# State-space stage of a twelve-stage decoder: the scan's input formed by differences, 1/A moved, boundary inputs apart

## The chip, the cores and the metric

The kernel runs on one core of a Trainium2 chip. The metric is the device time of one execution in microseconds (us): the median of three runs of the kernel before is 1734.0 us (1726.0 to 1737.9). One more execution was profiled; it took 1747.2 us.

## The reference

Twelve post-norm stages follow each other over x of 8 batches x 256 tokens x 128 dimensions. The change touches the seventh, a selective state-space layer with N = 16 states per dimension:

```python
BC = x @ W_in + b_in
Bm, Cm = (BC[..., :N], BC[..., N:])
dt = jax.nn.softplus((x @ W_dt1 + b_dt1) @ W_dt2 + b_dt2)
dt = jnp.clip(dt, 1e-07, 1000000.0)
tmp = A * dt[..., None]
A_bar = jnp.exp(tmp)
B_barX = jnp.expm1(tmp) / tmp * dt[..., None] * Bm[:, :, None, :] * x[..., None]

def combine(e1, e2):
    a1, b1 = e1
    a2, b2 = e2
    return (a1 * a2, a2 * b1 + b2)
_, h = jax.lax.associative_scan(combine, (A_bar, B_barX), axis=1)
return jnp.sum(h * Cm[:, :, None, :], axis=-1) + D * x
...
x = _layernorm(x + _L2_attn_ref(x, L2_attn_W_in, L2_attn_b_in, L2_attn_W_dt1, L2_attn_b_dt1, L2_attn_W_dt2, L2_attn_b_dt2, L2_attn_A, L2_attn_D), axis=-1)
```

So h(t) = a(t) h(t-1) + (a(t) - 1)/A B(t) x(t) for each dimension and state, with a = exp(A dt), and y sums C h over the 16 states.

## The kernel before

Each engine has its own hand-written program, and stages are Python functions named after the layer (L1f is the gated layer ahead, L2a the state-space stage, L2x the attention behind). Engines meet through counting semaphores; every engine runs its program strictly in the written order.

**The stage L2a.** Work is cut into 32 chunks t = 4 b + c: batch b, and four of the 16 states (c). A chunk is a tile of 128 dimensions x 1024, that is 4 states x 256 tokens. For each chunk:

- ScalarE (`scan_scaled`, L2475) multiplies the batch's tokens by the B of four states: eight 128x128 instructions. TensorE (`scan_inputs`, L1810) transposes them into PSUM banks 0-1 or 2-3, so that dimensions lie on partitions.
- ScalarE (`decays`, L2515 and L2516) writes a = exp(A dt) and tanh(A dt / 2), four instructions of 256 columns each. With them a - 1 is (a + 1) times the tanh.
- VectorE (`feed`, L3376) forms (a + 1) B x out of PSUM, GpSimd (`scan_gains`, L854 and L855) clears the decay of each first token and multiplies by the tanh.
- VectorE scans (L3384, both inputs in SBUF) and multiplies by C (L3388), which TensorE has spread over the partitions into banks 4-5 (`spread_c`, L1896: a 16-row selection matrix `SEL` times the rows of C, in fp32). Banks 4-5 exist once: chunk t's C is spread only after chunk t-1's product.
- TensorE sums the states into bank 6 (`summed`, L1912: eight matmuls of 128 columns against `by_state`, the identity over A) and adds D x (L1907). At the end of a batch VectorE reads y and adds x (`residual`, L3393), takes moments, GpSimd the root, and VectorE normalises (L3408).

**Preparation of a batch** runs inside the chunks of the two batches before it: transpose x (L1785), copy (L2435), project to C and to the low rank (L1790, L1791), copy with bias (L2445, L2446), step sizes and B (`scan_step_sizes`, L1796 and L1798), then on VectorE `scan_sized` (L3265, L3268: B and z), on ScalarE exp(-|z|) (L2453, L2455) and squares (L2462), on VectorE a series for softplus (L3275, L3278) and the clip (L3299, L3300). All of it passes through bank 7. Batches 0 and 1 are prepared inside L1f, between its own steps. The constants SCAN_... say at which chunk of the loop each piece stands; `due(t, offset, 4)` picks the batch.

The order on TensorE in the loop over chunks is: the inputs of chunk t + 2, the preparation due, C of chunk t, the sum of chunk t - 1. The order on VectorE is: feed of chunk t + 1, scan and product of chunk t, then the pieces due.

## Time and profile before

| | |
|---|---|
| median of 3 runs | 1734.0 us |
| profiled execution | 1747.2 us, of which the span is 1745.5 us |
| first scan of L2a starts | 765.1 us |
| reads of y, first to last batch | 799.5 to 973.1 us |
| VectorE, ScalarE, TensorE busy, 780 to 967 us | 177.1, 172.0, 173.5 of 187.0 us |

Times inside the profile are microseconds from the start of the span. PE is TensorE (PEld its weight loads), DVE VectorE, ACT ScalarE, POOL GpSimd. A float32 matmul stands as two records, one that reads fp32r as one, and a transpose as one. A row's `xN` counts instructions; the length of a timeline row covers all of them, and neighbours on one engine overlap by their start-up. Behind `|` a group row has busy us, the mean ns of one, and how long the engine stood idle before them, with what released it. PEclk is TensorE's granted clock as a share of 2.4 GHz; its two levels are 2.4 and 1.2 GHz.

### The profile page before, as it was taken

Reading aid. Unit: us, or ns where it says so; the run is one execution under the profiler, and the core shown is the slowest. Engines: PE = TensorE matmul, PEld = TensorE weight load, DVE = VectorE, ACT = ScalarE, POOL = GpSimd, SP = SyncE. Lnnn points to the kernel's source line nnn. Section 1 sums busy time; section 2 is a strip of 40 time slices with the busy share of each in tenths; the row PEclk is TensorE's granted clock in tenths of the full one; section 3 lists DMA queues with packets and bytes.
Section 4 is the critical chain, followed back from the end, with each engine's and each line's share of the span. In section 5 each row is a group of like instructions: output and inputs, shape, how many; then the busy total and the mean of one; then the engine's idle time right before and its main releaser. Section 6 shows DMA issues by size and latency. Waiting matters only on the chain.

```text
span 1745.5 us, 34465 instructions
## 1 busy us (share of the span) xinstructions
PE 1524.6 (87%) x12731; PEld 1091.4 (63%) x12741; DVE 1272.4 (73%) x2817; ACT 1068.0 (61%) x2219; POOL 693.3 (40%) x801
## 2 busy tenths in 40 slices
PE   6588778799998898899899999998889999989975
PEld 5344446578877555668678767665548984755542
DVE  2688862697775898479999677758854448758988
ACT  4499942367765676389999155547754443147765
POOL 3456536578887022356767313230000111511223
PEclk9799989899999999988988999999989998799985
DMA  3200121200000000010000100000000000000000
GB/s 133 111 13 14 42 87 39 59 10 2 1 1 1 2 2 2 4 37 1 2 1 1 58 2 2 2 13 2 1 2 1 1 1 11 0 19 2 2 1 25
DMA packets 14791, 30.94 MB, mean 18 GB/s; under 512 B 1537, under 2 KB 10145, under 8 KB 13857
## 3 DMA queue, kind: packets, MB, share of 16 engines
q1 hardware_dynamic: 13602, 26.63, 4.4%
q0 software_dynamic: 1024, 2.10, 0.4%
q8 instruction: 104, 1.70, 0.4%
q14 instruction: 61, 0.50, 0.1%
HBM read 22.42 MB, written 6.29 MB: 16 GB/s over the span
## 4 chain that ended last, share of the span: by engine, by line
PE 48%; ACT 14%; DVE 13%; POOL 13%; issue 11%; DMA 1%; another core or an unknown queue 0%; SPq 0%; POOLq 0%; DVEq 0%; ACTq 0%
PE PS L1420 5%; PE PS L1473 4%; ACT big L2262 4%; POOL big L837 4%; PE PS L1745 3%; DVE negmax L2803 3%; PE PS L1734 3%; POOL big L825 3%; ACT big L2240 2%; POOL big L833 2%; PE PS L1912 2%; PE PS L1495 2%; PE PS L1896 2%; PE PS L1325 2%; PE PS L1399 2%
## 5 line engine op out<-in xcount | busy, mean ns | idle before, releaser
L2240 ACT ACTIVATE big<-PS 128x1024 f32<-128x1024 f32 (+1 forms) x256 | 249.4, 975 | 160.3 <-PE PS L1427 159.8
L2803 DVE TENSOR_REDUCE negmax<-PS 128x4 f32<-128x1024 f32 x192 | 234.7, 1223 | 59.6 <-PE PS L1420 54.7
L1420 PE MATMUL PS<-KS,QS 32*128 32x256 f32 (+1 forms) x1152 | 134.4, 318 | 33.9 <-DVE negmax L2803 20.4
L1420 PEld LDWEIGHTS PS<-KS,QS 32*128 32x128 f32 x1152 | 88.0, 188 | 108.0 <-ACT big L2240 75.8
L711 POOL TENSOR_TENSOR rstd<-veps,mhalf 128x2 f32<-128x2 f32 x72 | 51.4, 714 | 241.3 <-DVE veps L2677 231.8
L1427 PE MATMUL PS<-QS,KS 32*128 32x256 f32 (+1 forms) x1152 | 134.7, 321 | 1.4 <-ACT big L2240 1.4
L1473 PE MATMUL PS<-big,V 128*32 128x256 f32 (+1 forms) x2048 | 134.9, 382 | 0.0
L737 POOL TENSOR_TENSOR res<-resb,XB 128x256 f32<-128x256 f32 x24 | 17.5, 728 | 254.7 <-ACT resb L2326 254.7
L779 POOL TENSOR_SCALAR KT<-QT 128x1024 f32<-128x1024 f32 x64 | 66.7, 1042 | 64.8 <-DVE QT L2822 62.9
L2822 DVE SCALAR_TENSOR_TENSOR QT<-PS,wint 128x1024 f32<-128x1024 f32 x64 | 77.3, 1219 | 16.1 <-PE PS L1365 15.5
L1427 PEld LDWEIGHTS PS<-QS,KS 32*128 32x128 f32 x1152 | 85.4, 188 | 5.5 <-issue 3.7
L825 POOL TENSOR_SCALAR big<-big,rsum 128x256 f32<-128x256 f32 (+1 forms) x144 | 61.2, 438 | 65.2 <-DVE rsum L2724 64.8
L2417 ACT ACTIVATE QT<-PS,W 128x256 f32<-128x256 f32 x128 | 53.5, 471 | 54.3 <-PE PS L1734 54.3
L837 POOL TENSOR_TENSOR big<-big 128x512 f32<-128x512 f32 x64 | 81.3, 1271 | 5.0
L1469 PE MATMUL PS<-big,V 128*32 128x512 f32 x512 | 63.4, 614 | 21.3 <-ACT big L2262 13.7
L1473 PEld LDWEIGHTS PS<-big,V 128*32 128x32 f32 x2048 | 54.4, 110 | 44.0 <-issue 15.3
L1129 PE MATMUL PS<-OT,W 128*128 128x256 f32 x272 | 74.5, 395 | 6.9 <-ACT QT L2188 6.9
L2188 ACT COPY QT<-PS 64x256 f32<-64x256 f32 x128 | 47.0, 367 | 53.3 <-DVE big L2708 51.7
L1912 PE MATMUL PS<-On,V 128*128 128x128 f32 x512 | 78.8, 319 | 0.0
L2262 ACT ACTIVATE big<-KT,W 128x1024 f32<-128x1024 f32 x64 | 73.0, 1141 | 8.9 <-POOL KT L779 8.9
L1912 PEld LDWEIGHTS PS<-On,V 128*128 128x128 f32 x512 | 73.1, 228 | 8.3 <-issue 8.3
L1896 PE MATMUL PS<-OT,SEL 16*128 16x256 f32 x256 | 67.0, 403 | 12.0 <-DVE V L3388 10.9
(479 smaller groups left out, 4331.5 us busy)
## 6 DMA issues: line engine op xcount, KB each, us to landing
W<-in_wpack SPq DMA_DIRECT2D x1, 4180.0 KB, 14.0
W<-in_wpack SPq DMA_DIRECT2D x1, 2560.0 KB, 8.9
W<-in_wpack SPq DMA_DIRECT2D x1, 2449.5 KB, 8.1
y_rows<-one_more SPq DMA_DIRECT2D x1, 2048.0 KB, 10.4
masks<-in_mask SPq DMA_DIRECT2D x8, 256.0 KB, 2.8
x_rows<-x_tok SPq DMA_DIRECT2D x16, 128.0 KB, 2.1
W<-in_wpack SPq DMA_DIRECT2D x1, 1538.0 KB, 6.1
x_tok<-in_x SPq DMA_DIRECT2D x1, 1024.0 KB, 5.0
```

The costliest lines, as they stand in the source:

```text
L825: ins = nc.gpsimd.tensor_scalar(PRW[:, u % 4, c0:c1], PRW[:, u % 4, c0:c1], rsum[:, u % 16, j:j + 1], 1.0, ALU.mult, ALU.mult)
L837: nc.gpsimd.tensor_tensor(q, q, RTW[:, u % 4, :, :], ALU.add).then_inc(sem("t_rope"), 1)
L1129: mm = nc.tensor.matmul(PS[:, QKB[u % 2], k * S:(k + 1) * S], w(f"{n}_w{x}", h * P, (h + 1) * P), OT[:, b, :], start=True, stop=True)
L1420: mm = nc.tensor.matmul(PS[:, MAXB[half], o], QS[r, bm % 2, tm, j * P:(j + 1) * P], KS[r, bm % 2, tm, k], start=not a.causal, stop=last)
L1427: mm = nc.tensor.matmul(PS[:, exp_banks(ge)[half], o], KS[r, be % 2, te, kb * P:(kb + 1) * P], QS[r, be % 2, te, q], start=not a.causal, s ...
L1473: mm = nc.tensor.matmul(out_rows[:, skip:S], v, PX[:, T % 2, h, kb * S:(kb + 1) * S - skip], start=first, stop=last)
L1896: mm = nc.tensor.matmul(PS[:, CB + k // 2, (k % 2) * S:(k % 2 + 1) * S], SEL[:, 4 * c + k, :], C_rows(b), start=True, stop=True)
L1912: mm = nc.tensor.matmul(PS[:, YB, j * P:(j + 1) * P], chunk("h", t)[:, at:at + P], by_state[:, 4 * c + k, :], start=False, stop=c == 3 and ...
L2240: nc.scalar.activation(PX[:, T % 2, 2 * p:2 * p + 2, 0:cols], PS[:, exp_banks(g)[0]:exp_banks(g)[0] + 2, 0:cols], ACT.Exp, scale=a.scale). ...
L2262: nc.scalar.activation((PX, PX2)[k][:, T % 2, 2 * p:2 * p + 2, :], clipped((QT, KT)[k], g), ACT.Exp, scale=a.scale, bias=w(("high_base", " ...
L2803: ins = nc.vector.tensor_reduce(negmax[:, h:h + 2, :].rearrange("p h j -> p (h j)"), banks.rearrange("p h (j k) -> p (h j) k", j=2), AX.X, ...
L2822: nc.vector.scalar_tensor_tensor(clipped(QT, g), PS[:, pair_banks(g):pair_banks(g) + 2, :], -100.0 / a.scale, capT[:, g // PAIRS % 2, :].u ...
```

## The change

The recurrence is rewritten. With v(t) = B(t) x(t), the sum w(t) = A h(t) + v(t+1) obeys w(t) = a(t) w(t-1) + v(t+1) - v(t), so the scan takes the plain decay and the differences of v, and y is the sum over states of (C/A) w minus x(t+1) times the sum over states of C(t) B(t+1) / A. Part by part:

- The tanh (16 a batch on ScalarE), the feed (4 a batch on VectorE) and GpSimd's product are gone. The scan reads its second input from PSUM banks 0-3, directly.
- The scaling of tokens 128 to 255 moves to GpSimd (`scan_scaled`, one 128x512 product a chunk); ScalarE keeps four of the eight.
- `scan_inputs` multiplies by `L2a_ahead` (difference of neighbouring tokens) instead of transposing: eight real float32 matmuls of 128 columns. It now waits for the scan of chunk t - 2, not for the feed, and stands last in TensorE's loop.
- The columns at tokens 127 and 255, which the matrix cannot form, and the first state are computed once a batch (three small matmuls in `scan_turn_x`, two small products on GpSimd in `scan_signed`, two in `scan_first_state`, one decay on ScalarE); `start(t)`, a ScalarE copy of 128x4x2, writes them into PSUM ahead of each scan. It stands behind the scaling and the decays in ScalarE's loop.
- 1/A moves into `SEL`, which has 64 rows (high and low parts of C and of 1/A) in fp32r and is built by VectorE in `scan_constants`; GpSimd's building of the old `SEL` at the start of the kernel goes. `summed` uses the identity as weights: four matmuls of 256 columns.
- C, B and the low rank come from one projection (`L2a_front`); ScalarE copies three pieces of it, and VectorE's new `scan_crossed_rows` makes the low part of C and C(t) B(t+1). `scan_step_sizes` overwrites that bank and so waits for it. z is written by ScalarE.
- At a batch's end: `cross` (matmul), `crossed_inputs` (VectorE), `read_y` (VectorE, in the place of the residual), `result` (two transposes) and `copy_result` (ScalarE), then the moments as before. The D x term carries x too.

```diff
+SCAN_START, SCAN_CROSS, SCAN_Y, SCAN_OUT, SCAN_STATS, SCAN_DONE = -2, 2, 4, 6, 7, 8
...
+                nc.gpsimd.tensor_tensor(chunk("x", t)[:, 512:1024].rearrange("p (k d) -> p k d", k=4),
+                                        x_tok[:, 2 * b + 1, :].unsqueeze(1).broadcast_to([P, 4, D]),
+                                        B_cols(b)[:, 16 + 4 * c:20 + 4 * c].unsqueeze(2).broadcast_to([P, 4, D]), ALU.mult)\
+                  .then_inc(sem("L2a_xs_second"), 1)
...
+                nc.gpsimd.tensor_tensor(starts(b)[:, 0:16], first_decay(b), starts(b)[:, 0:16], ALU.mult).then_inc(own, 1)
...
+                    nc.tensor.matmul(PS[:, 7, S:S + 32], x_tok[0:2, 2 * (b - 1), :], signed_B, start=True, stop=True)
+                    nc.tensor.matmul(PS[:, 7, S + 32:S + 48], x_tok[:, 2 * (b - 1), :], last_B, start=True, stop=False)
+                    mm = nc.tensor.matmul(PS[:, 7, S + 32:S + 48], x_tok[0:1, 2 * b - 1, :], B_cols(b - 1)[0:1, 16:32],
+                                          start=False, stop=True)
...
+                nc.tensor.matmul(PS[:, 7, 0:S], w("L2a_front"), xN(b), start=True, stop=True).then_inc(sem("L2a_psum"), 1)
 
             def scan_step_sizes(b):
-                pe.wait_ge(sem("L2a_bc"), b + 1)
-                nc.tensor.matmul(PS[:, 7, 0:S], w("L2a_wdt2", rows=64), low_rank, start=True, stop=True)
+                pe.wait_ge(sem("L2a_bc"), 2 * b + 2)
+                pe.wait_ge(sem("L2a_rows"), 2 * b + 1)
...
-                    pe.wait_ge(sem("L2a_fed"), t - 1)
...
+                    pe.wait_ge(sem("L2a_scan"), t - 1)
+                for k in range(8):
+                    bank, first = (0, 2)[t % 2] + k // 4, (k // 2 % 2) * S + (k % 2) * P
+                    mm = nc.tensor.matmul(PS[:, bank, first:first + P], chunk("x", t)[:, (k % 2 * 4 + k // 2) * P:(k % 2 * 4 + k // 2 + 1) * P],
+                                          w("L2a_ahead"), start=True, stop=True)
...
-                        mm = nc.tensor.matmul(PS[:, CB + k // 2, (k % 2) * S:(k % 2 + 1) * S], SEL[:, 4 * c + k, :], C_rows(b),
+                        mm = nc.tensor.matmul(PS[:, CB + k // 2, (k % 2) * S:(k % 2 + 1) * S], SEL[:, 4 * c + k, :], C_parts(b),
...
+                        nc.tensor.matmul(PS[:, YB, 0:S], diag, xN(b), start=True, stop=False)
+                    for k in range(4):
+                        mm = nc.tensor.matmul(PS[:, YB, 0:S], ident, chunk("h", t)[:, k * S:(k + 1) * S],
+                                              start=False, stop=c == 3 and k == 3)
+                    mm.then_inc(sem(f"{n}_summed"), 1)
...
+                    nc.tensor.matmul(PS[:, 7, 0:S], w_rows(f"{n}_AT", 32, 48), CB_rows(b), start=True, stop=True)\
+                      .then_inc(sem(f"{n}_turned_out"), 1)
...
+                        mm = nc.tensor.transpose(PS[:, result_bank(b), S + j * P:S + (j + 1) * P], summed_x[:, j * P:(j + 1) * P], ident)
...
+                for k in range(4):
+                    i = 4 * c + k
+                    ins = nc.scalar.activation(chunk("x", t)[:, k * P:(k + 1) * P], x_tok[:, 2 * b, :], ACT.Copy,
+                                               scale=B_cols(b)[:, i:i + 1])
...
+                        ins = nc.scalar.activation(chunk("decay", t)[:, k * S + 1:(k + 1) * S], step_size(b)[:, 1:S], ACT.Exp,
+                                                   scale=w(f"{n}_A", i, i + 1))
...
+                def start(t):
+                    b, c = t // 4, t % 4
+                    act.wait_ge(sem(f"{n}_xB"), t + 1)
...
+                    nc.scalar.copy(PS[:, bank:bank + 2, :].rearrange("p a c -> p (a c)").rearrange("p (k c) -> p k c", k=4)[:, :, 0:P:P - 1],
+                                   starts(b)[:, 16:48].rearrange("p (v k) -> p k v", v=2)[:, 4 * c:4 * c + 4, :])\
+                      .then_inc(sem(f"{n}_started"), 1)
...
+            def scan_crossed_rows(b):
+                dve.wait_ge(sem("L2a_bc"), 2 * b + 2)
...
+                nc.vector.scalar_tensor_tensor(CB_rows(b)[:, 0:S - 1], PS[32:48, 7, 1:S], w_rows("L2a_bfront", 32, 48),
+                                               CB_rows(b)[:, 0:S - 1], ALU.add, ALU.mult).then_inc(sem("L2a_rows"), 1)
...
+                        scan_crossed_rows(0)
...
-                scan_states(6, 16)
...
-                def feed(t):
-                    dve.wait_ge(sem(f"{n}_decay"), t + 1)
...
-                    nc.vector.scalar_tensor_tensor(fed_to(t), chunk("decay", t), 1.0, flat(PS[:, bank:bank + 2, :]),
-                                                   ALU.add, ALU.mult).then_inc(sem(f"{n}_fed"), 1)
...
-                    nc.vector.tensor_tensor_scan(h, chunk("decay", t), chunk("gain", t), 0.0, ALU.mult, ALU.add)\
+                    h, bank = chunk("h", t), (0, 2)[t % 2]
+                    nc.vector.tensor_tensor_scan(h, chunk("decay", t), flat(PS[:, bank:bank + 2, :]), 0.0, ALU.mult, ALU.add)\
...
+                def crossed_inputs(b):
+                    dve.wait_ge(sem(f"{n}_turned_out"), 2 * b + 1)
+                    nc.vector.tensor_tensor(crossed[:, 0:S - 1], PS[:, 7, 0:S - 1], xN(b)[:, 1:S], ALU.mult)\
+                      .then_inc(sem(f"{n}_y_read"), 1)
...
+                    nc.vector.tensor_tensor(summed_x, PS[:, 6, 0:S], crossed, ALU.subtract).then_inc(sem(f"{n}_y_read"), 1)
```

What TensorE runs over one and a half chunks in the middle of the stage, before: C (L1896), sums (L1912), inputs (L1810) and step sizes (L1796, L1798).

```order
L1896 MATMUL PS<-OT,SEL 128x256 [waits L2a_hc,L2a_bc]
L1896 MATMUL PS<-OT,SEL 128x256 x3
L1912 MATMUL PS<-On,V 128x128 [waits L2a_hc]
L1912 MATMUL PS<-On,V 128x128 x7
L1810 MATMUL PS<-W,QT 128x128 [waits L2a_fed,L2a_xs]
L1810 MATMUL PS<-W,QT 128x128 x7
L1796 MATMUL PS<-OT,W 128x256 [waits L2a_bc]
L1798 MATMUL PS<-W,KT 128x16 x2
L1896 MATMUL PS<-OT,SEL 128x256 [waits L2a_hc]
L1896 MATMUL PS<-OT,SEL 128x256 x3
```

And after, from C (L1977) of one chunk on: D x (L1987), sums (L1989), step sizes (L1877, L1879), inputs (L1891).

```order
L1977 MATMUL PS<-KS,SEL 128x256 [waits L2a_hc]
L1977 MATMUL PS<-KS,SEL 128x256 x3
L1987 MATMUL PS<-KT 128x256 [waits L2a_y_read,L2a_hc]
L1989 MATMUL PS<-V,W 128x256 x4
L1877 MATMUL PS<-OT,W 128x256 [waits L2a_rows,L2a_bc]
L1879 MATMUL PS<-W,KT 128x16 x2
L1891 MATMUL PS<-W,QT 128x128 [waits L2a_scan,L2a_xs_second,L2a_xs]
L1891 MATMUL PS<-W,QT 128x128 x7
L1977 MATMUL PS<-KS,SEL 128x256 [waits L2a_hc]
L1977 MATMUL PS<-KS,SEL 128x256 x3
L1989 MATMUL PS<-V,W 128x256 [waits L2a_hc]
```

The inputs stand behind the step sizes now and wait for L2a_scan where they waited for L2a_fed; the sums are four wide matmuls, and L1877 waits for L2a_rows too.

In L1f, around the step sizes of batch 1, TensorE ran this before (L1844 narrows and L1834 widens the gated layer, L1796 and L1798 are the step sizes):

```order
L1844 MATMUL PS<-big,QT 128x128 [waits var,L1f_h]
L1844 MATMUL PS<-big,QT 128x128 x5
L1834 MATMUL PS<-QT,big 128x256 [waits L1f_h]
L1834 MATMUL PS<-QT,big 128x256 x2
L1796 MATMUL PS<-OT,W 128x256 [waits L2a_bc]
L1798 MATMUL PS<-W,KT 128x16 x2
L1834 MATMUL PS<-QT,big 128x256 [waits L1f_silu,xT]
L1834 MATMUL PS<-QT,big 128x256 x2
L1844 MATMUL PS<-big,QT 128x128 [waits var,L1f_h]
```

And it runs this after (L1925, L1915; L1877 and L1879 are the step sizes):

```order
L1925 MATMUL PS<-big,QT 128x128 [waits var,L1f_h]
L1925 MATMUL PS<-big,QT 128x128 x5
L1915 MATMUL PS<-QT,big 128x256 [waits L1f_h]
L1915 MATMUL PS<-QT,big 128x256 x2
L1877 MATMUL PS<-OT,W 128x256 [waits L2a_rows,L2a_bc]
L1879 MATMUL PS<-W,KT 128x16 x2
L1915 MATMUL PS<-QT,big 128x256 [waits L1f_silu,xT]
L1915 MATMUL PS<-QT,big 128x256 x2
L1925 MATMUL PS<-big,QT 128x128 [waits var,L1f_h]
```

Only the wait for L2a_rows is new. It is given by L3402, the second row of `scan_crossed_rows`, which stands on VectorE in L1f behind the gated product (L3466), the rest of the series (L3422) and the clip (L3451, L3452):

```order
L3466 TENSOR_TENSOR QT<-QT,PS 128x768 [waits y,L1f_silu,L1f_h_psum]
L3422 SCALAR_TENSOR_TENSOR xs<-masks,xs 128x256 [waits L2a_q]
L3422 SCALAR_TENSOR_TENSOR xs<-masks,xs 128x256 [waits L2a_q,t_dve]
L3451 SCALAR_TENSOR_TENSOR OT<-OT,xs 128x256 [waits L2a_series]
L3452 SCALAR_TENSOR_TENSOR KT<-OT,KT 128x256 [waits t_dve]
L3400 SCALAR_TENSOR_TENSOR KS<-PS,W,KS 32x256 [waits L2a_bc]
L3402 SCALAR_TENSOR_TENSOR one_more<-PS,W,one_more 16x255
L3410 TENSOR_TENSOR rt<-PS,W 128x32 [waits L2a_psum]
```

Nothing moved past it; the two rows L3400 and L3402 were put between the clip and `scan_sized` (L3410).

ScalarE's order over one chunk after the change: the four scalings (L2583), the decays (L2626), the start copy (L2636), then z (L2561, L2562) and exp(-|z|) (L2564).

```order
L2583 ACTIVATE QT<-x_tok,rt 128x128 [waits L2a_xB,L2a_rows]
L2583 ACTIVATE QT<-x_tok,rt 128x128 x3
L2626 ACTIVATE big<-KT,W 128x255 [waits L2a_scan]
L2626 ACTIVATE big<-KT,W 128x255 x3
L2636 COPY PS<-KT 128x4x2 [waits L2a_xB]
L2561 ACTIVATE KT<-PS,W 128x256 [waits L2a_dt,L2a_series,L2a_rows]
L2562 ACTIVATE OT<-PS,W 128x256
L2564 ACTIVATE KT<-KT 128x256 [waits L2a_u]
L2583 ACTIVATE QT<-x_tok,rt 128x128 [waits L2a_xB]
```

The start copy of the next chunk can be reached only behind the z of this one, which waits for L2a_rows from VectorE.

## Rows read from the trace of the kernel before

**Rows 1.** Engine busy time by stretch; the first row names the columns
```profile
core 0: us, PE busy (x) PEld busy (x) DVE busy (x) ACT busy (x) POOL busy (x), PEclk, DMA share, GB/s
780.00:807.00 27.00, 27.00 (x141) 22.89 (x141) 24.11 (x27) 25.87 (x74) 17.58 (x10) 0.76 0.01 2
...
860.00:887.00 27.00, 23.02 (x146) 18.35 (x145) 25.81 (x30) 25.86 (x74) 18.24 (x11) 0.99 0.00 1
...
780.00:967.00 187.00, 173.49 (x1008) 143.98 (x1008) 177.12 (x189) 172.00 (x489) 130.81 (x72) 0.90 0.00 1
```

**Rows 2.** Groups by line, 800 to 950 us: operation, shapes, count, busy us, mean ns, idle
```profile
L2475 ACT ACTIVATE QT<-x_tok,rt 128x128 f32<-128x128 f32 x186 | 56.6, 386 | 0.0
...
L3384 DVE TENSOR_TENSOR_SCAN V<-big 128x1024 f32<-128x1024 f32 x23 | 52.5, 2283 | 0.0
...
L1896 PE MATMUL PS<-OT,SEL 16*128 16x256 f32 x184 | 48.6, 406 | 7.7 <-DVE V L3388 7.7
...
L3376 DVE SCALAR_TENSOR_TENSOR one_more<-big,PS 128x1024 f32<-128x1024 f32 x12 | 14.6, 1217 | 4.2 <-ACT big L2516 4.2
...
L3278 DVE SCALAR_TENSOR_TENSOR xs<-masks,xs 128x256 f32<-128x256 f32 x20 | 12.7, 636 | 0.5
```

**Rows 3.** Timeline: start us, length us, engine, line, operation, count, idle before
```profile
855.30 2.28 DVE L3384 TENSOR_TENSOR_SCAN V<-big 128x1024 f32<-128x1024 f32 x1
...
855.50 4.23 POOL L855 TENSOR_TENSOR big<-big,one_more 128x1024 f32<-128x1024 f32 x1
...
859.37 0.42 ACT L2453 ACTIVATE KT<-OT 128x256 f32<-128x256 f32 x1 [1.04 <-DVE OT L3268]
```

**Rows 4.** Timeline, the reads of y of the first, sixth and last batch
```profile
799.51 0.42 DVE L3393 TENSOR_TENSOR res<-PS,x_tok 128x256 f32<-128x256 f32 x1
...
933.81 0.42 DVE L3393 TENSOR_TENSOR res<-PS,x_tok 128x256 f32<-128x256 f32 x1
...
973.05 0.42 DVE L3393 TENSOR_TENSOR res<-PS,x_tok 128x256 f32<-128x256 f32 x1 [2.72 <-PE PS L1912]
```

**Rows 5.** Chain that ended last, in order of time: start us, length us, what
```profile
741.95 1.30 PE PS L1834 x6
...
780.41 3.61 PE PS L1912 x16
...
784.02 0.88 PE PS L1810 x8
785.11 1.92 PE PS L1896 x8
787.03 1.98 PE PS L1912 x16
...
863.90 0.40 ACT big L2516
```

**Rows 6.** Timeline of TensorE, matmuls in fp32r (four row tiles of 32 rows)
```profile
1000.24 0.73 PE L1325 MATMUL PS<-HL,spread_by 32*128 32x256 f32 x8
```

**Rows 7.** Timeline, the gated stage ahead, where the first two batches are prepared
```profile
728.45 0.24 DVE L3292 RECIPROCAL negmax<-W 128x16 f32<-128x16 f32 x1
...
733.61 0.70 PE L1796 MATMUL PS<-OT,W 64*128 64x256 f32 x2
...
734.44 0.42 DVE L3313 COPY QT<-PS 128x256 f32<-128x256 f32 x1
...
748.63 0.70 PE L1796 MATMUL PS<-OT,W 64*128 64x256 f32 x2
...
751.30 0.48 DVE L3300 SCALAR_TENSOR_TENSOR KT<-OT,KT 128x256 f32<-128x256 f32 x1
```

**Rows 8.** Timeline, the first two scans of the stage
```profile
764.70 2.58 POOL L855 TENSOR_TENSOR big<-big,wint 128x1024 f32<-128x1024 f32 x1
...
765.11 4.32 DVE L3384 TENSOR_TENSOR_SCAN V<-big 128x1024 f32<-128x1024 f32 x1
...
777.14 1.22 DVE L3388 TENSOR_TENSOR V<-V,PS 128x1024 f32<-128x1024 f32 x1
```

## What I expect of the change

> **What bounds the kernel now.** I read the stage of the change alone, since the other eleven run the same instructions. The reads of y by VectorE mark the batches [rows 4]: five batches from 799.51 to 933.81 us take 134.3, a period of 26.86 us, and the last two together, when nothing is left to prepare, 39.24. Then the busy time by stretch [rows 1]: VectorE 25.81 of 27 us, ScalarE 25.86, TensorE 23.02 where its clock is 0.99. In the stretch where TensorE is granted 0.76 it is busy for all of 27.00 us, and VectorE still gets through 24.11 us of work. So VectorE and ScalarE set the pace, locked together: VectorE's feed waits for ScalarE's tanh (4.2 us of idle in its group, [rows 2]), and ScalarE waits 1.04 us for VectorE's z [rows 3]. GpSimd has room. A change must relieve VectorE and ScalarE both to shorten the period, and then TensorE is next.
>
> **VectorE, a batch.** Now 25.7 (25.81 on 26.86 us). Removed: four feeds of 1.22 us [rows 2], 4.9, and z's addition, 0.4 (as a read of y, 128x256 out of PSUM, [rows 4]). Added: two rows of crossed C and B and the product with the next token, 0.42 each by the same row, 1.3. That is 21.7. The scan's price from PSUM is in no row. It is 2.28 us for 1024 elements with both inputs in SBUF [rows 2]; the same columns out of PSUM cost the feed 1.22, so PSUM can be read at twice the scan's pace, and I take 2.28. Below it there is nothing to gain, as its recurrence sets its pace at nearly double the feed's; above it I keep 4.32, the longest scan of the trace [rows 8], as the bound.
>
> The trace shows VectorE and GpSimd holding each other up: the product on GpSimd takes 4.23 us beside a scan that began 0.2 us earlier, and 2.58 where it began first, while the scan then takes 4.32 instead of 2.28 [rows 3, 8]. The series of softplus pays for it too: 636 ns in the mean [rows 2] against 0.48 for a like instruction in L1f [rows 7]. GpSimd's share falls from 4.2 us a chunk to about 1.3 (half of 2.58, for 512 columns), so I take 1.0 us a batch off: 20.7. The Trainium skill (SBUF — State Buffer, "SBUF: two separate sides") says that a VectorE instruction with two SBUF inputs and a GpSimd instruction that reads SBUF exclude each other, the later one waiting to the end; the trace agrees, 4.32 against 2.28. By that rule the new scan, with one input in PSUM, is never held, which adds nothing to my sum, as steady scans were not held before either.
>
> Waits come on top. With the product of chunk t-1 as zero: TensorE has spread C at 0.6, summed at 2.3 and projected the coming batch at 2.8; ScalarE's three copies end at 4.1; VectorE is through scan, product and read of y at 3.9, so the crossed rows wait some 0.3. A chunk later ScalarE does z and its exponential (1.2), scalings (1.2), decays (1.6) and start copy (0.3) after `scan_sized`, 4.3 us, while VectorE has 3.5 us of scan and product: 0.8 more. The crossed input waits 0.3 for `cross`. With 0.2 for the hand-overs: 1.6. **VectorE: 22.3 a batch.**
>
> **ScalarE, a batch.** Of 25.7, sixteen tanh of 0.40 [rows 5] and sixteen scalings of 0.30 (56.6 us for 186, [rows 2]) go: 11.3. z's copy, one copy more of the projection, the first decay and the result are 0.4 each, and four start copies and one of 48 columns at most 0.4 each: 3.6 at most. 18.0, no bound any more. What it can still do is be late: inputs of a chunk 2.0, scalings and decays 2.8, start copy 0.3, scan 2.3, in all 7.4 for every second chunk, less than two chunks of 5.6.
>
> **TensorE, a batch, at 2.4 GHz.** Before: inputs 0.88, C 1.92, sums 1.98 [rows 5], four times, 19.1, and 3.1 for preparation and D x: 22.2. The inputs are now like the sums before, 16 records of 128 columns, 1.98. The new sums are eight records of 256 columns; six of that shape take 1.30 [rows 5], so 1.73. C in fp32r has four records with 64 rows: below, the 0.73 for eight 32-row matmuls [rows 6] gives 0.09 each, but those are on four row tiles; above, 0.24 each, the old rate. I take 0.14, nearer the lower one as the type is the same, 0.56. A chunk is 4.27, four are 17.1. Preparation loses one projection (0.5) and gains the three small matmuls (0.8), `cross` (0.5) and the two result transposes (0.3): 4.2. Sum 21.3. In the stretch at clock 0.76 the 22.2 took 27.0, a rate of 0.82; at the stage's mean of 0.90 [rows 1] that makes 0.925. **TensorE: 23.0 a batch.**
>
> Banks 4-5 exist once, and the inputs now wait for the scan, so one engine's lateness is not made good by the other's slack. I add 0.5 to the larger: **a period of 23.5 us for 26.86.**
>
> **Ends of the stage.** L1f gets later. First, VectorE's constants end at 728.7 now [rows 7]; the selection matrix of 2048 columns (2.4, twice the feed) and five small ones bring that to about 732.4, and ScalarE's copies and the next silu wait for it. The step sizes of batch 0, at 733.61, then stand behind crossed rows that end at about 736.9: 3.3 late. Second, those of batch 1, at 748.63, wait for crossed rows behind the clip, which ends at 751.78: 752.7, that is 4.1 more. Third, the first inputs stand ahead of the last narrow product, 1.98 for 0.88: 1.1. In all 8.5. Against it the feeds, GpSimd's products and the held scan drop out: the product of chunk 1, which ends at 778.4 [rows 8], comes at 776.9 by my count, 1.5 earlier. If none of the L1f waits were hidden worse or better, this is net; its bounds are 7 earlier and 7 later. From there to the first read of y, 21.1 us before, now three chunks of 5.9: 3.5. Five periods: 16.8. The last two batches: 14.0 of scan and product each, with 5.0 and 2.5 beside them, 35.5 for 39.24: 3.7. The end of the last batch is longer by transposes and a copy: 1.0. The larger weights and the selection matrix that GpSimd no longer builds at the start lie beside other work, at worst 1 us.
>
> Sum: 1.5 + 3.5 + 16.8 + 3.7 - 1.0 = 24.5 us less than the profiled 1747.2. That execution is 13.2 above the median of the runs; I take the difference off the median: **1734.0 - 24.5 = 1709.5 us.**
>
> **Rivals.** Each puts another period P into the same sum.
>
> *TensorE stays at the high clock, P = 22.3.* For it: the new period leaves it fewer gaps, and eight transposes a chunk become real matmuls. Against: it fell to 0.76 while busy for 27.00 of 27.00 [rows 1]. P = 22.3 gives 1.5 + 4.4 + 22.8 + 5.5 - 1.0 = 33.2, 1701 us; chance 0.15. The Trainium skill (TensorE: Matmul & The Clock Gate, "Part 4: PE-mode transpose") says that transposes do not count as activity of the engine for its clock; that would speak for this rival, and the row at 0.76, with its eight transposes a chunk, does not contradict it.
>
> *TensorE becomes the plain bound, P = 25.5.* If the whole stage ran as the stretch at 0.76 did, 21.3 would take 25.9, and half a clock's chain of sums (3.61 for 1.98, [rows 5]) delays C each time. Gain 1.5 + 2.0 + 6.8 + 0.7 - 1.0 = 10.0, 1724 us; chance 0.20.
>
> *The scan is slower out of PSUM: slower than before.* Place: every chunk on VectorE. At 4.3 us it adds 8.1 a batch, P = 30.3, and the sum turns to 25 us more, 1759. It decides from about 3.4 us on (P = 26.9, no gain), and costs over 1% from about 4.1. For it only that no row shows such a scan; against it the feed's rate. Chance 0.08. The Trainium skill (VectorE: DVE Perf Modes, "Why PSUM operands drop a tier") caps a float32 instruction with a PSUM operand at one element a cycle; the scan is below that already, so by the page it keeps its time.
>
> *Nothing changes.* The pace is kept by a hand-over that I read as slack, P = 26.8, and L1f's delays eat the start: about 1733. Every engine's busy time falls except TensorE's, so this is weak: 0.07.
>
> **Numbers.** The forecast (1703 to 1716) has 0.50. The range is 1698 to 1726: it takes in the first two rivals and leaves out the scan's upper bound, the case of no change and a little beyond each end. A measurement of this kernel can tell about 1%, 17 us: faster by more than that 0.66 (the forecast and the first rival, and a little), within it 0.24, slower 0.10.
>
> **What would show it.** The new reads of y should be 23 to 24 us apart, scans 2.3 us, GpSimd's products below 2.3, the C matmuls near 0.6 a chunk, no idle of ScalarE that counts. Wrong: scans above 3 us; a period above 25 with TensorE busy throughout (second rival) or with VectorE idle ahead of scans for the start copy (my waits too small); the step sizes of batch 1 in L1f with no wait ahead of them; a first scan after 775 us.

## The result, and the profile after

| | before | after |
|---|---|---|
| median of 14 runs | 1734.5 us (1726.0 to 1738.6) | 1723.5 us (1712.5 to 1729.1) |
| profiled execution, its span | 1747.2, 1745.5 us | 1728.7, 1726.8 us |
| ratio after to before | | 0.9936, 95% interval 0.9917 to 0.9955 |

The kernel is 0.64% faster, some 11 us, where 24.5 us had been forecast. The two profiled executions stand 18.5 us apart, which looks like most of the forecast and isn't. To see that, the span is cut at two marks that both kernels have: VectorE's residual of batch 1 in the gated stage L1f (723.69 us before, 722.11 after), and the last norm of the state-space stage (975.38 and 961.71). Ahead of the first mark the new execution is 1.6 us shorter, behind the second 5.0 us, in stages that run the same instructions (but for GpSimd's building of the old `SEL`, which is gone at the start). That is scatter: in the experiments below, which leave those stages alone, the first mark lies anywhere from 719.7 to 728.5 us. Between the marks, where the change is, it is 251.7 - 239.6 = 12.1 us shorter. That is the number to explain, and it agrees with the 11 us of the medians.

| between the marks, us | before | after | difference | forecast |
|---|---|---|---|---|
| residual of batch 1 to residual of batch 7 in L1f ("tail") | 33.4 | 48.0 | +14.6 | +8.5 |
| from there to the first read of y | 42.4 | 33.6 | -8.8 | -13.5 |
| five periods | 134.3 | 118.9 | -15.4 | -16.8 |
| last two batches | 39.2 | 35.9 | -3.3 | -3.7 |
| last read of y to last norm | 2.3 | 3.2 | +0.9 | +1.0 |
| sum | 251.7 | 239.6 | -12.1 | -24.5 |

The steady state came out as forecast. The reads of y of the first, sixth and last batch, from the timeline of VectorE after (start, length, line; answers to [rows 4]):

```profile
803.72 0.42 DVE L3540 TENSOR_TENSOR XB<-PS,XB 128x256 f32<-128x256 f32 x1 [0.63 <-PE PS L1989]
...
922.62 0.42 DVE L3540 TENSOR_TENSOR XB<-PS,XB 128x256 f32<-128x256 f32 x1
...
958.51 0.42 DVE L3540 TENSOR_TENSOR XB<-PS,XB 128x256 f32<-128x256 f32 x1
```

The groups by line, 800 to 950 us (busy us, mean ns | idle before, and what ended it; answers to [rows 2]):

```profile
L3524 DVE TENSOR_TENSOR_SCAN V<-big,PS 128x1024 f32<-128x1024 f32 x27 | 61.6, 2281 | 0.5 <-PE PS L1989 0.3
L1891 PE MATMUL PS<-W,QT 128*128 128x128 f32 x426 | 55.1, 283 | 6.8 <-DVE V L3524 6.8
...
L2583 ACT ACTIVATE QT<-x_tok,rt 128x128 f32<-128x128 f32 x100 | 31.9, 390 | 16.7 <-PE PS L1891 16.7
L886 POOL TENSOR_TENSOR QT<-x_tok,rt 128x512 f32<-128x512 f32 x25 | 26.0, 1039 | 85.4 <-PE PS L1891 84.6 <-DVE x_tok L3554 0.7
...
L3422 DVE SCALAR_TENSOR_TENSOR xs<-masks,xs 128x256 f32<-128x256 f32 x22 | 11.0, 501 | 0.7
```

The scan takes 2281 ns with its input in PSUM, against 2283 from SBUF. The series of softplus (L3422) fell from 636 to 501 ns, and GpSimd's product takes 1.04 us. ScalarE waits 16.7 us for TensorE's inputs in this window, and TensorE 6.8 us for the scan. The windows of single batches show who sets the pace (columns as in [rows 1]):

```profile
851.10:874.41 23.31, 22.20 (x136) 18.71 (x136) 20.14 (x28) 16.92 (x51) 5.96 (x10) 1.00 0.00 1
874.41:899.31 24.90, 23.79 (x136) 20.21 (x136) 20.13 (x27) 17.04 (x51) 5.96 (x10) 0.93 0.01 1
899.31:922.62 23.31, 22.19 (x136) 18.41 (x136) 20.13 (x28) 16.34 (x49) 5.96 (x10) 1.00 0.01 1
```

TensorE is busy for 22.20 of 23.31 us, VectorE for 20.14, ScalarE for 16.9. Before, four of the five periods were 26.8 us, whether the granted clock was 1.00 or 0.87 (the fifth, at 0.87, was 27.25): VectorE and ScalarE hid it. Two of the kernel before:

```profile
799.51:826.29 26.78, 26.72 (x151) 22.14 (x151) 25.25 (x29) 25.65 (x74) 18.15 (x10) 0.87 0.00 1
...
853.04:879.80 26.76, 22.79 (x146) 18.25 (x145) 25.57 (x30) 25.65 (x75) 18.09 (x10) 1.00 0.01 2
```

Now the batch at 0.93 takes 24.90 us and its neighbours 23.31. The timeline of TensorE shows that both batches have the same gap of 1.11 us, ahead of the inputs that wait for the scan. Behind the gap at 881.16 us the same sixteen records take 3.48 us, behind the one at 857.84 they take 2.02:

```profile
857.84 2.02 PE L1891 MATMUL PS<-W,QT 128*128 128x128 f32 x16 [1.11 <-DVE V L3524]
...
881.16 3.48 PE L1891 MATMUL PS<-W,QT 128*128 128x128 f32 x16 [1.11 <-DVE V L3524]
...
885.36 1.99 PE L1989 MATMUL PS<-V,W 128*128 128x256 f32 x8
```

What failed is the start. The rows of L1f and of the first chunks after (answers to [rows 7, 8]):

```profile
736.40 1.19 PE L1877 MATMUL PS<-OT,W 64*128 64x256 f32 x2 [4.95 <-DVE one_more L3402]
...
738.39 2.91 PE L1915 MATMUL PS<-QT,big 128*128 128x256 f32 x6
...
758.42 1.05 PE L1877 MATMUL PS<-OT,W 64*128 64x256 f32 x2 [4.21 <-DVE one_more L3402]
...
760.28 2.91 PE L1915 MATMUL PS<-QT,big 128*128 128x256 f32 x6
...
762.98 2.66 PE L1925 MATMUL PS<-big,QT 128*128 128x128 f32 x12
...
772.54 1.68 POOL L1054 TENSOR_SCALAR x_tok<-res,mv,rstd 128x128 f32<-128x128 f32 x2
...
774.79 0.17 ACT L2636 COPY PS<-KT 128x8 f32<-128x8 f32 x1 [2.15 <-POOL KT L909]
...
775.16 2.29 DVE L3524 TENSOR_TENSOR_SCAN V<-big,PS 128x1024 f32<-128x1024 f32 x1 [2.38 <-ACT PS L2636]
...
784.93 2.90 PE L1891 MATMUL PS<-W,QT 128*128 128x128 f32 x16 [1.13 <-DVE V L3524]
...
787.76 1.22 PE L1977 MATMUL PS<-KS,SEL 64*128 64x256 f32 x4
...
788.91 3.78 PE L1989 MATMUL PS<-V,W 128*128 128x256 f32 x8
```

TensorE waits 4.95 us ahead of the step sizes of batch 0 and 4.21 us ahead of those of batch 1, each time for VectorE's crossed rows. Behind each wait it works at the lower clock: six widening records take 2.91 us, against 1.54 before, and the narrow product behind the second wait 2.66 against 1.50. The start copy (L2636) then waits 2.15 us for GpSimd's first state, which stands behind the last normalisation (L1054), and holds up the first scan. A third stretch at the low clock follows at 784.93: 2.90, 1.22 and 3.78 us for inputs, C and sums, which take 2.02, 0.74 and 1.99 at the high clock.

### The profile page after: what moved, and what is told of

Same layout as the page of the kernel before. It is cut to its first block, busy times and chain, and to the rows that moved or that the text cites. A ratio compares the mean times of both kernels' runs of the same rounds, so it can differ in the third digit from the quotient of the medians.

```text
span 1726.8 us, 34149 instructions
## 1 busy us (share of the span) xinstructions
PE 1509.5 (87%) x12661; PEld 1083.3 (63%) x12661; DVE 1231.5 (71%) x2790; ACT 997.9 (58%) x2035; POOL 594.2 (34%) x800
## 3 DMA queue, kind: packets, MB, share of 16 engines
q0 software_dynamic: 1024, 2.10, 0.4%
## 4 chain that ended last, share of the span: by engine, by line
PE 49%; DVE 13%; POOL 13%; issue 12%; ACT 11%; DMA 1%; SPq 0%; POOLq 0%; DVEq 0%; ACTq 0%
PE PS L1488 5%; PE PS L1541 4%; POOL big L866 4%; ACT big L2361 4%; PE PS L1813 3%; DVE negmax L2938 3%; PE PS L1802 3%; POOL big L854 3%; PE PS L1891 3%; ACT big L2339 2%; PE PS L1989 2%; PE PS L1563 2%; POOL big L862 2%; PE PS L1391 2%; PE PS L1467 2%
## 5 line engine op out<-in xcount | busy, mean ns | idle before, releaser
L2516 ACT ACTIVATE QT<-PS,W 128x256 f32<-128x256 f32 x128 | 53.6, 470 | 55.8 <-PE PS L1802 55.8
L1537 PE MATMUL PS<-big,V 128*32 128x512 f32 x512 | 64.5, 622 | 22.9 <-ACT big L2361 15.4
L1541 PEld LDWEIGHTS PS<-big,V 128*32 128x32 f32 x2048 | 54.2, 110 | 44.1 <-issue 15.4
L3524 DVE TENSOR_TENSOR_SCAN V<-big,PS 128x1024 f32<-128x1024 f32 x32 | 73.0, 2281 | 2.9 <-ACT PS L2636 2.4
L2361 ACT ACTIVATE big<-QT,W 128x1024 f32<-128x1024 f32 x64 | 72.8, 1138 | 2.9 <-DVE QT L2957 2.9
L1891 PE MATMUL PS<-W,QT 128*128 128x128 f32 x480 | 62.8, 286 | 9.1 <-DVE V L3524 9.1
```

Source lines behind the costliest of these rows:

```text
L1541: mm = nc.tensor.matmul(out_rows[:, skip:S], v, PX[:, T % 2, h, kb * S:(kb + 1) * S - skip], start=first, stop=last)
L1891: mm = nc.tensor.matmul(PS[:, bank, first:first + P], chunk("x", t)[:, (k % 2 * 4 + k // 2) * P:(k % 2 * 4 + k // 2 + 1) * P], w("L2a_ahea ...
L2361: nc.scalar.activation((PX, PX2)[k][:, T % 2, 2 * p:2 * p + 2, :], clipped((QT, KT)[k], g), ACT.Exp, scale=a.scale, bias=w(("high_base", " ...
L3524: nc.vector.tensor_tensor_scan(h, chunk("decay", t), flat(PS[:, bank:bank + 2, :]), 0.0, ALU.mult, ALU.add)\
```

## The experiments

All are edits of the changed kernel. The measures are read in the profiled execution of each, in us from the first mark; they repeat to about 0.1 us, as the executions' tails of 47.99 in the kernel after, with the third edit and with the seventh show, while the medians scatter by several. "Behind" is the span behind the second mark. Where only one time is given, it was run once.

| kernel | tail | first scan | first read of y | last norm | behind | time, median |
|---|---|---|---|---|---|---|
| before | 33.4 | 41.4 | 75.8 | 251.7 | 770.1 | 1734.5 |
| after | 48.0 | 53.1 | 81.6 | 239.6 | 765.1 | 1723.5 |
| e1_rows | 40.8 | 45.8 | 74.4 | 232.4 | 754.7 | 1712.4 |
| e2_consts | 47.3 | 52.3 | 79.3 | 238.9 | 764.9 | 1731.4 |
| e3_state | 48.0 | 50.8 | 77.0 | 236.6 | 768.3 | 1730.9 |
| e4_all | 39.7 | 43.5 | 70.4 | 230.1 | 754.0 | 1720.7 of 6 |
| e5_keep | 42.3 | 47.4 | 72.7 | 230.8 | 762.3 | 1717.5 |
| e6_pe | 48.1 | 53.1 | 81.9 | 257.5 | 760.9 | 1741.9 |
| e7_act | 48.0 | 53.1 | 81.1 | 256.1 | 754.8 | 1741.3 |
| e8_first | 39.0 | 44.1 | 69.4 | 229.1 | 761.9 | 1712.5 |
| e9_order | 32.9 | 36.8 | 65.3 | 223.3 | 751.1 | 1698.2 of 5 |
| e10_fill | 48.5 | 53.6 | 79.0 | 235.4 | 749.3 | 1710.8 |
| e11_best | 33.3 | 37.2 | 62.6 | 219.0 | 764.3 | 1707.4 of 5 |
| e12_shift | 33.4 | 37.2 | 62.6 | 222.6 | 758.8 | 1705.0 of 6 |

### e1_rows: the crossed rows of batch 1 earlier

```diff
 ScalarE, L1f:  elif b == 5: ... scan_scaled(0)
+                   scan_projected(1)
-               elif b == 6: scan_projected(1)
 VectorE, L1f:  for b in range(2, B):
+                   if b == 6: scan_crossed_rows(1)
                    gated_residual(b - 1)
                    gated_product(b)
 ...            elif b == 6: ... scan_softplus(0)
-                   scan_crossed_rows(1)
                    scan_sized(1)
```

> Edit: in the gated stage ScalarE projects batch 1 one silu earlier and VectorE computes its crossed rows ahead of the residual of batch 5, so that TensorE finds them done at the step sizes of batch 1. Measures are taken from the residual of batch 1 in the gated stage: to the residual of batch 7 (tail; 33.4 us before, 48.0 after the change) and to the first read of y (75.8 and 81.6). Theory A, TensorE's waits in the gated stage and the low clock behind each are what is lost: the wait of 4.2 us goes and the 2.9 and 2.7 us of low-clock work behind it fall to 1.5 each, so the tail is 41 to 42.5 and the first read of y 75 to 76.5. Theory B, the gated stage carries more work of VectorE and TensorE and the wait only moves: tail 46.5 or more. Theory C, the first scan is set by GpSimd's first state and ScalarE's decays, not by the tail: tail near 42, but the first read of y at 79.5 or later.

The rows end at 754.66 us and TensorE goes on at 755.36 without a wait, at the high clock (timelines of VectorE and TensorE):

```profile
754.18 0.48 DVE L3402 SCALAR_TENSOR_TENSOR one_more<-PS,W,one_more 16x255 f32<-16x255 f32 x1
...
755.36 0.70 PE L1877 MATMUL PS<-OT,W 64*128 64x256 f32 x2
...
756.45 1.54 PE L1915 MATMUL PS<-QT,big 128*128 128x256 f32 x6
```

Tail and first read of y are both 7.2 us earlier: 4.2 of wait and 3.0 of low clock. Theory A holds, with 0.2 and 0.6 us more than its ranges allowed; B and C don't: a microsecond of the tail comes through to the reads of y.

### e2_consts: the constants later

```diff
 def scan_constants(): ... memsets
+    line.wait(); dve.sem_inc(dve_consts, 1)
+def scan_matrices():            # called in L1f at b == 4
     reciprocal, SEL, diag ...
 ScalarE: wait for dve_consts moved from scan_projected(0) to the squares of batch 0
```

> Edit: VectorE's selection matrix, reciprocals and D matrix (4.6 us) are computed two batches later, where VectorE is idle for 2.9 us, and ScalarE waits only for the small constants, and only ahead of its squares. Measures from the residual of batch 1 in the gated stage: tail 48.0, first read of y 81.6 after the change. Theory A: TensorE's wait of 4.95 us ahead of the step sizes of batch 0 shrinks to 1 or less and the low-clock work behind it (1.2, 1.0, 2.9 us) runs in 0.7, 0.6, 1.6, while the late matrix costs up to 2: tail 42.5 to 45, first read of y 76.5 to 79. Theory B, the same work only moves: tail 47 or more. Theory C: tail as A, first read of y 80 or later.

The tail shrank by 0.7 us only; here my theory A was wrong and B right. The constants did hold the crossed rows, but not alone. In the kernel after, ScalarE's copies, which the rows read, wait for the semaphore behind the constants (L3445); here they wait only for the projection (timelines of ScalarE, the kernel after, then this one):

```profile
731.63 0.46 ACT L2551 ACTIVATE one_more<-PS,W 16x256 f32<-16x256 f32 x1 [8.40 <-DVEq L3445]
```

```profile
730.22 0.47 ACT L2551 ACTIVATE one_more<-PS,W 16x256 f32<-16x256 f32 x1 [3.47 <-PE PS L1870]
```

The rows end 11.0 us behind the first mark in place of 14.2. VectorE now idles 2.7 us ahead of the residual of batch 2, and the rows still stand behind residual, product and copy. TensorE waits 2.32 us in place of 4.95, and its clock falls all the same:

```profile
735.25 0.42 DVE L3464 COPY QT<-PS 128x256 f32<-128x256 f32 x1
...
736.19 0.47 DVE L3403 SCALAR_TENSOR_TENSOR one_more<-PS,W,one_more 16x255 f32<-16x255 f32 x1
...
736.81 0.81 PE L1877 MATMUL PS<-OT,W 64*128 64x256 f32 x2 [2.32 <-DVE one_more L3403]
...
738.43 2.91 PE L1915 MATMUL PS<-QT,big 128*128 128x256 f32 x6
```

At their new place the 4.8 us of constants made the product of batch 5 late, and TensorE waited 1.13 us there. The residual of batch 3 is 2.4 us earlier than in the kernel after, that of batch 4, behind the constants, only 0.3: the gain was made and lost again.

### e3_state: GpSimd's first state earlier

```diff
 GpSimd, L1f:
+    if b == 7: scan_first_state(0)
     inverse_root(n, b); ... x_tok
 GpSimd, L2a:
-    scan_first_state(0)
```

> Edit: GpSimd computes the first state of batch 0 ahead of its last normalisation in the gated stage instead of behind it. Measures from the residual of batch 1: tail 48.0, first scan 53.0, first read of y 81.6 after the change. Theory A: tail unchanged (within 0.5); the start copy waited 2.15 us for GpSimd, so the first scan is 50.5 to 51.5 and the first read of y 79 to 80.5. Theory C, this order is the main thing: the first read of y at 78 or earlier. Theory D, something else is as late as GpSimd there (C's spread, the filler matmuls): first read of y stays within 0.7 of 81.6.

The first scan comes 2.2 us earlier, as theory A said, and waits 0.17 us now. The first read of y comes 4.6 us earlier, at 77.0; by that number theory C (78 or earlier) was met and A's 79 to 80.5 was not. But only 2.2 us of it are shown to be GpSimd's order. The rest came with the third stretch of low clock, which is not there, though the gap ahead of it still is: the inputs of chunk 3, 2.90 us in the kernel after, take 2.02.

```profile
771.99 0.22 POOL L909 TENSOR_TENSOR KT<-KT 128x16 f32<-128x16 f32 x1
...
775.07 2.29 DVE L3525 TENSOR_TENSOR_SCAN V<-big,PS 128x1024 f32<-128x1024 f32 x1 [0.17 <-DVE xs L3423]
...
785.63 2.02 PE L1892 MATMUL PS<-W,QT 128*128 128x128 f32 x16 [1.13 <-DVE V L3525]
```

### e4_all: the three together

> The three edits together. Theory A: tail (33.4 before, 48.0 after the change) 36 to 39, first read of y 68 to 72 from the residual of batch 1, and the steady periods as they are (23.3 to 24.9): 10 to 13 us less than the changed kernel, 1711 to 1714 us, a ratio to the kernel before of 0.986 to 0.988. Theory B: tail 44 or more and at most 4 us less, 1719.5 or more. Theory C alone: 2 to 4 us less as well, all of it behind the tail.

First read of y 11.2 us and last norm 9.5 us earlier than in the kernel after. The first read, at 70.4, is inside theory A's range, the tail of 39.7 just above its 36 to 39 and far below theory B's 44. The median is 1720.7 us beside 1737.9 of the kernel before on the same chip, a ratio of 0.9896 (0.9863 to 0.9930). The median did less than the stage: 7 us less than after by the ratios, not 10 to 13, and above A's 1711 to 1714.

### e5_keep: no order changed, TensorE kept busy in its waits

```diff
 TensorE, L1f:  elif b in (3, 6):
+    pe.wait_ge(sem("var"), before("L1f", "var") + b - 1)
+    for _ in range(20 if b == 3 else 17):
+        nc.tensor.matmul(PS[:, (OUTB, FB_BANK)[b % 2], 0:512], identb, causal[0:512], start=True, stop=True)
     scan_step_sizes(b // 6)
```

> Edit: nothing but filler matmuls on TensorE (bf16, 512 columns, results overwritten) where it waits in the gated stage: 20 ahead of the step sizes of batch 0 and 17 ahead of those of batch 1, each about 0.23 us, so about as long as the waits of 4.95 and 4.2 us. All waits of the kernel stay. Theory A, the clock falls behind each wait and the work behind it costs 2.3 and 2.5 us more for that: the first widening product behind each takes 1.5 instead of 2.9 us, tail 43 to 44.5 instead of 48.0. Rival, the clock there is low for another reason, or the fillers themselves are late: the widening products stay above 2.5 us and the tail at 47 or more.

The first wait ends 14.3 us behind the mark in both kernels; the second ends 2.4 us earlier, as nothing ahead of it ran at the low clock. TensorE comes out of both at the high clock: the widening products behind take 1.54 us.

```profile
730.75 4.48 PE L1960 MATMUL PS<-causal,identb 128*128 128x512 bf16 x20
...
736.52 0.67 PE L1877 MATMUL PS<-OT,W 64*128 64x256 f32 x2 [1.29 <-DVE one_more L3406]
...
737.58 1.54 PE L1915 MATMUL PS<-QT,big 128*128 128x256 f32 x6
...
751.72 3.83 PE L1960 MATMUL PS<-causal,identb 128*128 128x512 bf16 x17
...
756.10 0.67 PE L1877 MATMUL PS<-OT,W 64*128 64x256 f32 x2 [0.55 <-DVE one_more L3406]
```

The tail is 5.7 us shorter (42.3, a little better than theory A's 43) and the first read of y 8.9 us earlier, with 37 matmuls more and every wait of the kernel still in place. So of the 14.6 us by which the tail grew, 5.7 are low clock; the other 3.2 us up to the first read of y are the third stretch, which is gone here too. That the fillers took it away is not shown: the gap ahead of it, 1.11 to 1.13 us, is the same in eight versions, with a low stretch behind it in five (the kernel after, e1_rows, e2_consts, e4_all, e9_order) and none in three (e3_state, e5_keep, e8_first).

### e6_pe and e7_act: who sets the new pace

```diff
 e6, TensorE, scan_inputs(t):
+    for _ in range(4 if t >= 2 else 0): mm = nc.tensor.matmul(... the last one again ...)
 e7, ScalarE, scan_scaled(t):
+    for k in range(4 if t >= 2 else 0): nc.scalar.activation(big[:, 4096 + ...], x_tok[:, 2 * b, :], ACT.Copy, scale=...)
```

> Edit: TensorE repeats the last input matmul of each chunk from the third on four times (128 columns, about 0.12 us each): 0.49 us a chunk, 2.0 a batch at full clock; nothing else is changed. Steady period of the changed kernel 23.3 us with one of 24.9. Theory P, TensorE is the bound of the new steady state: the period grows by 1.8 to 2.8, to 25.1 to 26.6. Rival Q, the pace is set by a chain through VectorE and ScalarE and TensorE has slack: by 1.0 or less.

> Edit: ScalarE scales four more times a chunk from the third on (128 columns, about 0.3 us each, into unused memory), 1.2 us a chunk, 4.8 a batch. Theory P, ScalarE has slack in the steady state (it was busy for 61% of it): the period grows by less than 1.5. Rival Q, its lateness sets the start copies and through them the scans: the period grows by 3 or more, with VectorE idle ahead of the scans for the start copy.

With e6 every period but the last two is 26.3 to 26.4 us, 3.1 more than the 23.3 of a batch at the high clock. A float32 matmul is two records, so the four repeats were eight, 0.9 us a chunk and not the 0.49 that I had put down. In a whole batch TensorE is busy for 25.77 us instead of 22.20, 3.6 more, and its gap shrinks from 1.11 to 0.66 us, which leaves the 3.1. Theory P holds: TensorE is the bound.

```profile
830.02:856.45 26.43, 25.77 (x167) 22.29 (x166) 20.65 (x26) 17.04 (x51) 5.97 (x10) 1.00 0.00 1
```

With e7 the periods are 26.1 to 27.3, by 2.5 to 4.0 longer than the high-clock batches of the kernel after: ScalarE, which had been idle for a quarter of the time, costs as much as TensorE. Two batches show how. In the first, TensorE has the high clock throughout, and the period still grows from 24.07 to 26.55: the gap ahead of the inputs is 1.90 us for 1.10, a gap of 1.06 stands ahead of the inputs of the last chunk, where there was none, and one scan waits 0.90 us for the start copy.

```profile
809.64:836.19 26.55, 23.60 (x145) 19.76 (x144) 20.67 (x26) 23.78 (x73) 5.95 (x10) 1.00 0.01 1
```

```profile
817.90 2.02 PE L1891 MATMUL PS<-W,QT 128*128 128x128 f32 x16 [1.90 <-DVE V L3528]
...
869.80 2.84 PE L1891 MATMUL PS<-W,QT 128*128 128x128 f32 x16 [1.89 <-DVE V L3528]
...
872.57 1.22 PE L1977 MATMUL PS<-KS,SEL 64*128 64x256 f32 x4
...
873.72 3.78 PE L1989 MATMUL PS<-V,W 128*128 128x256 f32 x8
```

In the last three of the five the clock falls behind the gap of 1.89 us (granted 0.87 to 0.88), TensorE is busy for 3.2 us more, the second gap is gone, and the period is 27.3, 4.0 more. So ScalarE's lateness alone cost 2.5 us; if it is worth the same in the slow batches, the low clock adds about 1.5 there, an estimate. Theory P is wrong: ScalarE's idle time was no slack. Theory Q's growth of 3 or more came in three batches of five; its sign, a scan that waits for the start copy, only in the first.

### e8_first: the crossed rows of batch 0 ahead of the residual

```diff
 VectorE, L1f:  for b in range(2, B):
+                   if b == 3: scan_crossed_rows(0)
                    gated_residual(b - 1)
 ...            elif b == 3:
-                   scan_crossed_rows(0)
                    scan_sized(0)
+                   scan_matrices()      # SEL and diag only
 ScalarE: wait for dve_consts moved from scan_projected(0) to the squares of batch 0
```

> Edit, for batch 0 alone: VectorE computes its crossed rows ahead of the residual of batch 2, where it idled for 2.7 to 3.3 us, instead of behind residual, product and copy; the selection and D matrices (2.6 us) stand behind the column copy of B of batch 0, the reciprocals stay; ScalarE no longer waits for the matrices. Measures from the residual of batch 1 in the gated stage: tail 48.0, first read of y 81.6 after the change; 47.3 and 79.3 when the constants alone were moved. Theory A, the place of the crossed rows in VectorE's order is what makes TensorE wait ahead of the step sizes of batch 0, not the constants as such: no wait above 0.5 us there, the widening product behind it in 1.5 to 1.6 us, tail 41.5 to 43.5 and first read of y 74.5 to 77. Rival B, the work of the gated stage only moves: tail 46 or more.

The rows end at 727.78 us, before TensorE wants them, and it neither waits nor slows:

```profile
727.30 0.48 DVE L3403 SCALAR_TENSOR_TENSOR one_more<-PS,W,one_more 16x255 f32<-16x255 f32 x1
...
729.01 0.70 PE L1877 MATMUL PS<-OT,W 64*128 64x256 f32 x2
...
730.10 1.54 PE L1915 MATMUL PS<-QT,big 128*128 128x256 f32 x6
```

The tail is 9.0 us shorter, better than expected, though the wait for batch 1 (4.21 us) is still there. This run changes two things: the place of the rows, and, as in e2_consts, ScalarE's wait for the constants, whose matrices (2.6 us) now stand behind `scan_sized`. Counted from the mark, the rows end at 14.2 us in the kernel after, at 11.0 with the constants moved, and at 8.1 here; TensorE wants them at 9.3. So each of the two is worth about 3 us, and only both together removed the wait and the low clock behind it. The order alone was not run: with the old wait, ScalarE's copies would not be there for rows at that place.

### e9_order: orders alone

> Edit: the order of the run before for batch 0, the early crossed rows of batch 1 and GpSimd's first state ahead of its last normalisation, together; only orders and waits, no instruction added or left out. Measures from the residual of batch 1: tail 33.4 before, 48.0 after the change, 39.7 with the first three edits; first read of y 75.8, 81.6, 70.4. Theory A: TensorE waits nowhere for more than 1.5 us in the gated stage and keeps the high clock: tail 35 to 37, first read of y 65.5 to 68, the last norm at 225 to 228 (239.6 after the change), and 1708 to 1713 us in the median where the changed kernel has 1723.5. Rival B: tail 38.5 or more, 1717 or more.

The tail is 32.9 us, shorter than the kernel before had without the added work, and the last norm at 223.3. The median is 1698.2 us (1695.3 to 1699.6) beside 1732.6 of the kernel before, a ratio of 0.9800 (0.9781 to 0.9820), 10 us below what theory A expected. This is the fastest version measured, but not all of it is the stage. Between the marks it is 16.3 us shorter than the kernel after; behind them its profiled execution took 751.1 us for 765.1, with the same instructions. The last experiment, whose stage is as short, has 0.9819 (0.9777 to 0.9861). Windows of all engines, 725 to 765 us, first of the kernel after and then of this one:

```profile
725.00:765.00 40.00, 30.84 (x145) 25.86 (x144) 21.29 (x59) 16.13 (x33) 13.80 (x20) 0.80 0.00 1
```

```profile
725.00:765.00 40.00, 39.29 (x244) 33.25 (x243) 30.48 (x78) 28.88 (x68) 24.23 (x32) 0.98 0.10 34
```

TensorE is busy for 39.3 of 40 us where it had been for 30.8, at a clock of 0.98 for 0.80. (The same stretch of time is not the same work: this run is already in L2a at its end.)

### e10_fill, e11_best, e12_shift: filling the steady gap

```diff
 e10, TensorE, L2a, behind scan_step_sizes(b):
+    for _ in range(8): nc.tensor.matmul(PS[:, YB, 0:S], identb, zeros, start=False, stop=False)
 e11 = e9 + e10
 e12 = e11, and ahead of the last result:
+    for _ in range(21): nc.tensor.matmul(PS[:, 0, 0:512], identb, causal[0:512], start=True, stop=True)
```

> Edit: the changed kernel with eight filler matmuls a batch (bf16, 256 columns of zeros added to the running sum, about 0.12 us each) behind the step sizes, where TensorE idles for 1.11 us in every batch waiting for the scan. Theory A, a period of 24.9 where its neighbours have 23.3 is one in which the clock fell behind this gap: with the gap filled all five periods are 23.2 to 23.6, and the stretch of 7.9 us of low clock behind the second such gap, ahead of the first read of y, goes too (first read of y 77 to 78.5 from the residual of batch 1, for 81.6). Rival: the falls have nothing to do with this gap, one or two of the five periods are still above 24.5; or the fillers delay the work, all periods 24.0 or more.

The fillers end at 787.40 us and the gap is 0.24 us; all five periods are 23.3 to 24.1 (the first with 24.07 as in the kernel after, above theory A's 23.6), none of 24.9. The first read of y is 2.6 us earlier, for 3.2 gained and 0.5 lost, at 79.0, half a microsecond above A's range.

```profile
786.37 1.03 PE L2026 MATMUL PS<-wint,identb 128*128 128x256 bf16 x8
...
787.64 2.02 PE L1891 MATMUL PS<-W,QT 128*128 128x128 f32 x16 [0.24 <-DVE V L3527]
```

> Edit: all orders of e9 and the fillers of e10. Theory A: the gains add: first read of y 65 to 68 from the residual of batch 1, every period 23.2 to 23.6, 1706 to 1711 us, a ratio to the kernel before of 0.981 to 0.985. Rival: the fillers give nothing over e9 (within 1 us in stage time).

In the stage the gains add, the first read of y at 62.6 where 65 to 68 had been expected: 4.3 us less than with the orders alone, the last norm at 219.0. The median is 1707.4 us, within theory A's 1706 to 1711, though 9.3 us more than e9_order. Behind the stage its profiled execution took 764.3 us and that of e9_order 751.1. Later stages run the same instructions in both, at different clocks: in this stretch at a granted clock of 0.99 in the one and 0.90 in the other (windows of 120 us, first e9_order, then e11_best, which lies some microseconds further back in its work; the kernel after has 0.89 there, the kernel before 0.87):

```profile
1440.00:1560.00 120.00, 109.40 (x964) 72.96 (x962) 92.95 (x174) 56.00 (x93) 35.83 (x37) 0.99 0.03 8
```

```profile
1440.00:1560.00 120.00, 111.63 (x873) 75.80 (x871) 86.10 (x161) 49.87 (x84) 35.07 (x36) 0.90 0.03 8
```

> The run with orders and fillers has a stage 4.3 us shorter than the run with the orders alone (last norm at 218.98 for 223.32 us from the residual of batch 1), and yet a median 9.3 us longer; behind the stage its profiled execution needs 764.3 us where the other needs 751.1, by stretches of low clock in the later stages, which run the same instructions. Edit: 21 filler matmuls (bf16, 512 columns, about 0.23 us each) on TensorE ahead of the last result of the stage, so that the stage ends about 4.2 us later, at 223.2, as with the orders alone. Theory F, the clock falls in the later stages depend on the time at which those stages are reached: the later stages need 749 to 753 us again and the median is 1696 to 1702, though 4 us of idle work were added. Theory R, they vary from one run or chip to the next: the median is that of the run with fillers plus 4.2, 1709 to 1714, and the span behind the stage is anywhere between 749 and 770, the bounds of the profiled executions so far.

The stage ended where that of e9_order ends, at 222.6, and the later stages took 758.8 us, not 751. The six runs were 1696.0, 1696.1, 1703.1, 1706.8, 1708.2 and 1708.8 us, on both sides. Theory F's 749 to 753 did not come back with the phase, and theory R's median, 1709 to 1714, wasn't reached either. What stands is that one program finds the later stages faster or slower from run to run; whether e11_best has worse odds than e9_order or had bad luck in five runs is open.

## Why the prediction was right or wrong

**The bound and the period: right, by two errors that cancel.** VectorE's term was good: scan 2.28 us, series relieved; busy for 20.1 us a batch where 20.7 stood before the waits. The third rival (a scan slower from PSUM) is dead. ScalarE's 18.0 at most is 16.9. TensorE's 21.3 us at full clock measured 22.2: C's four fp32r matmuls take 0.67 us (876.45 minus 875.78) and not 0.56, which is half of it, and the sums take 1.83 (887.19 minus 885.36) for 1.73. The way of adding up was short before the change too: 22.2 by the prediction's rows, where a batch at the high clock is busy for 22.79. Its clock was taken as 0.925 of full and was 1.00 in four batches of five. So I had 23.0 from 21.3 and a low clock, and it was 22.2 and a gap of 1.1; with the half microsecond for hand-overs that is 23.5 against 23.3 measured, 23.8 in the mean of five. The first rival said that the clock would rest high with real matmuls in place of the transposes, and it did. That the transposes were the reason is not shown: the kernel before had a batch at 1.00 with the same transposes. The Trainium skill (TensorE: Matmul & The Clock Gate, "Part 4: PE-mode transpose"), which the rival cited, says that a transpose does not count as the engine being busy in the same way; this trace neither confirms nor contradicts it. The period it put on that, 22.3, was too short, as TensorE itself was longer. The second rival's mechanism, TensorE as the bound, is what e6_pe shows, at a better clock. Its time, 1724 us, is what was measured, by luck: its period of 25.5 did not come, and what it charged to the five periods was lost at the start.

**The last two batches and the end: right**, 3.3 for 3.7 and 0.9 for 1.0.

**The start: wrong, and it is most of the error.** "First read of y" was to come 5.0 us earlier and came 5.8 later, 10.8 of the 12.4 us missed. One of the signs of being wrong that the prediction had named is in the trace, a first scan after 775 us (775.16). The other for the start is not: the step sizes of batch 1 do wait, 4.21 us, as forecast. Three steps went wrong.

- *The tail, +8.5.* Both waits were named and their lengths were near (3.3 forecast and about 4.4 measured as lateness of the step sizes of batch 0; 4.1 and 4.21). What the term left out is TensorE's clock behind a wait: 5.7 us by e5_keep, and 14.6 less 5.7 is 8.9, close to the 8.5. The sum counted TensorE's work in L1f at the rate of before, though [rows 1] held a stretch at 0.76 to warn of it.
- *From the tail to the first read, -13.5, of which 4.7 were missed.* GpSimd's first state behind its last normalisation cost the first scan 2.2 us (e3_state). The prediction never priced that new wait: it took GpSimd for an engine with room, and asked how busy it is, not where its instruction stands. The rest is mostly the third stretch at the low clock, behind a gap of 1.13 us: with that gap filled, the way from the tail to the first read is 3.2 us shorter (e10_fill).
- *Attribution inside the first term.* I put batch 0's lateness down to the constants alone. They account for about 3 of the 6 us by which the rows could come earlier; the other 3 are the place of the rows behind residual, product and copy. Moving the constants gained 0.7 us (e2_consts), moving both 9.0 (e8_first).

**The offset of the profile.** The sum was taken off the median, and that was sound. By the two profiled executions alone, 18.5 us apart, the forecast would have looked nearly right; 6.6 us of that lie outside the marks.

**Sensitivity to the clock was not forecast at all.** The kernel before ran a batch in 26.8 us at 0.87, 0.94 and 1.00 alike (one at 0.87 took 27.25). Making TensorE the bound made each fall of the clock cost: 1.6 us in a steady batch. The Trainium skill (TensorE: Matmul & The Clock Gate, "A second HAM failure mode: psum-queue depth-cycling") says that short idles between groups of matmuls make the clock go down and up again; the fall behind the gap at 881.16 us agrees with it, but the neighbouring batches of 23.31 us have the same gap of 1.11 us without a fall, and what tells them apart is open.

## What to carry to other kernels

When a change makes TensorE the bound, price each wait ahead of it twice: the wait, and the work behind it at half the clock. Here that was 4.2 and 3.0 us for one wait. Where a new instruction is waited for, look at what stands ahead of it on its engine, and ahead of what it reads, before looking at how long it is: moving the constants alone gave 0.7 us, moving them and two instructions of 0.48 us gave 9.0. Reordering alone (e9_order) shortened the stage by 16.3 us, more than the 12.1 that the change itself had brought. And cut the span at marks on both sides of the change, since the stages around it moved the profiled time by 6.6 us here.

## What the runs showed of the hardware

- TensorE's clock can fall behind a gap, and the length of the gap does not alone decide it. Behind waits of 2.3 to 6.2 us ahead of the step sizes it was low each time. Behind 1.9 us it was low in three of four batches (e7_act), behind 1.11 us in one or two of the five steady batches of each kernel with that gap, behind the 1.25 us of the next batch, and behind 0.66 and 0.24 us (e6_pe, e10_fill, e11_best), in none. The low stretches read lasted from about 3 to 8 us.
- Matmuls whose results are thrown away buy time: 37 of them in two waits gained 5.7 us in the tail (e5_keep, one profiled execution).
- A scan with its second input in PSUM keeps its pace, 2281 ns for 1024 elements against 2283.
- Four fp32r matmuls of 64 rows and 256 columns take 0.67 us, about 0.17 each, nearly twice the 0.09 of 32-row ones on four row tiles [rows 6].
- The same instructions behind the stage took 749 to 770 us in fourteen profiled executions; where windows were compared, it went with the granted clock.
